# Two scan steps of a pair as one scan of 1024 columns, in the tiles in which a sequence begins

## The reference

```python
def _selective_scan(u, delta, A, Bm, Cm, D_param):
    def step(h, inp):
        delta_t, B_t, C_t, u_t = inp
        dA = jnp.exp(delta_t[:, :, None] * A[None])
        dBu = (delta_t * u_t)[:, :, None] * B_t[:, None, :]
        h = dA * h + dBu
        y_t = jnp.einsum('bdn,bn->bd', h, C_t)
        return (h, y_t)
    ...                       # h starts at zero in each sequence
    return y + u * D_param[None, None, :]

x = _layernorm(x + lightning_attention(x))   # layer 0, gated, 16 heads
x = _layernorm(x + ffn_0(x))                 # silu(x W1) * (x W3), Hadamard, W2
x = _layernorm(x + _selective_scan(...))     # layer 1, 32 states for each feature
x = _layernorm(x + ffn_1(x))                 # silu gate, 512 -> 2048 -> 512
```

## Time and profile before

| | us |
|---|---|
| median of 3 runs | 1828.31 (1827.86 to 1829.96) |
| profiled execution, its own time | 1820.48 |
| its span, first to last instruction | 1818.7 |
| scans of tile 0, first start to last start | 538.6 to 803.5 |
| first start of a scan in tile 1 | 808.1 |
| scans of tile 2, first start to last start | 1087.3 to 1363.8 |
| PE busy | 1736.3 (95%) |
| DVE busy | 1241.6 (68%) |
| mean granted clock of TensorE, share of full | 0.994 |

### The profile page before, as it was taken

How to read it: one execution, slowest core, us unless ns; L and a number is a source line. 1 busy time by engine, 2 the same in 40 slices (tenths; PEclk the granted TensorE clock), 3 DMA queues, 4 the chain that set the end, 5 groups by cost and what they waited for, 6 DMA issues and landing times. The chain is left out here.

```text
span 1818.7 us, 26882 instructions
## 1 busy us (share of the span) xinstructions
PE 1736.3 (95%) x9472; PEld 1134.8 (62%) x9472; DVE 1241.6 (68%) x1336; ACT 1120.5 (62%) x1721; POOL 1194.6 (66%) x932
## 2 busy tenths in 40 slices
PE   7999999799989999999999999998999999999998
PEld 5666666577756665565555665554656566667786
DVE  2524443323139999999899999987999999982212
ACT  5453443566577777867767777676776767653212
POOL 4634433355528877899887997788987988772111
PEclk9999999999999999999999999999999999999999
DMA  7443423487858987788776997777877787864652
GB/s 254 135 130 97 148 65 126 170 297 260 298 169 297 320 310 268 256 294 307 249 258 239 318 311 259 241 262 248 279 283 275 261 276 261 290 225 165 206 194 93
DMA packets 160023, 427.07 MB, mean 235 GB/s; under 512 B 31888, under 2 KB 54992, under 8 KB 159504
## 3 DMA queue, kind: packets, MB, share of 16 engines
q1 hardware_dynamic: 159888, 425.34, 68.6%
HBM read 356.07 MB, written 69.21 MB: 234 GB/s over the span
## 5 line engine op out<-in xcount | busy, mean ns | idle before, releaser
L1885 POOL TENSOR_TENSOR q_or_raw_or_h_times_c<-h_states,c_rep 128x512 f32<-128x512 f32 x293 | 375.5, 1296 | 50.0 <-DVE h_states L1775 45.2
L1650 ACT ACTIVATE decay<-delta_on_states,a_neg 128x512 f32<-128x512 f32 x512 | 350.2, 716 | 44.2 <-DMA delta_on_states<-delta 39.9
L1760 DVE TENSOR_TENSOR du_spread_in_d_b<-du_spread_in_d_b,b_rep 128x1024 f32<-128x1024 f32 x256 | 310.3, 1212 | 30.8 <-PE du_spread_in_d_b L1472 28.3
L1775 DVE TENSOR_TENSOR_SCAN h_states<-decay,h_last,du_spread_in_d_b 128x512 f32<-128x512 f32 x256 | 317.7, 1270 | 9.0 <-ACT h_last L1655 2.3
L1885 POOL TENSOR_TENSOR h_times_c_rest<-h_states,c_rep 128x512 f32<-128x512 f32 x219 | 282.2, 1300 | 55.7 <-DVE h_states L1775 47.6
L1775 DVE TENSOR_TENSOR_SCAN h_states<-decay,du_spread_in_d_b 128x512 f32<-128x512 f32 x256 | 302.2, 1209 | 18.4 <-ACT h_last L1655 12.3
L1837 POOL TENSOR_TENSOR h_lo<-v_or_silu_in_h_lo,h_hi 128x512 fp32r<-128x512 f32 x128 | 166.9, 1304 | 204.3 <-ACT h_hi L1552 203.3
L111 PE MATMUL y_or_aux<-h_hi,w 128*128 128x512 f32 x468 | 193.9, 414 | 10.9 <-POOL h_lo L1837 10.7
L1725 DVE TENSOR_TENSOR v_or_silu_in_h_lo<-v_or_silu_in_h_lo,up_or_scores 128x512 f32<-128x512 f32 x128 | 86.9, 679 | 146.0 <-PE up_or_scores L113 131.5
L113 PE MATMUL y_or_aux<-h_hi,w 128*128 128x512 f32 x468 | 183.4, 392 | 0.0
L112 PE MATMUL y_or_aux<-h_lo,w 128*128 128x512 f32 x468 | 182.8, 391 | 0.0
(11 more groups left out here) (240 smaller groups left out, 3840.0 us busy)
## 6 DMA issues: line engine op xcount, KB each, us to landing
delta_on_states<-delta SPq DMA_DIRECT2D x256, 512.0 KB, 5.8
w<-w_split SPq DMA_DIRECT2D x112, 512.0 KB, 5.6
attn_w_hi_or_x_hi_w<-w_split SPq DMA_DIRECT2D x112, 512.0 KB, 5.2
attn_w_lo_or_x_lo_w<-w_split SPq DMA_DIRECT2D x112, 512.0 KB, 5.4
w_split<-w_presplit_hi_lo SPq DMA_DIRECT2D x32, 512.0 KB, 4.0
w_presplit_hi_lo<-in_w13b SPq DMA_DIRECT2D x32, 256.0 KB, 3.5
w_split<-attn_w_hi_or_x_hi_w SPq DMA_DIRECT2D x8, 1024.0 KB, 6.6
w_split<-attn_w_lo_or_x_lo_w SPq DMA_DIRECT2D x8, 1024.0 KB, 6.6
```

Of the source, the lines that this page charges most:

```text
L1650: act.activation(da[:, s % ND], dring[:, s % NR], ACT.Exp, scale=a[:, column(s):column(s) + 1]).then_inc(s_da, 1)
L1760: dve.tensor_tensor(both, both, brep[:, tile_of(s // SPO) % 2].unsqueeze(1).to_broadcast([P, 2, TT]), ALU.mult).then_inc(s_db, 1)
L1775: dve.tensor_tensor_scan(hs[:, s % NH], da[:, s % ND], uu[:, s % NU], initial, ALU.mult, ALU.add).then_inc(s_hs, 1)
L1885: pool.tensor_tensor(hc[s % NC_], hs[:, s % NH], crep[:, tile_of(s // SPO) % 2], ALU.mult).then_inc(s_hc, 1)
```

## The change

In the tiles in which a sequence begins (0 and 2), one `tensor_tensor_scan` over 1024 columns, `scan_both`, takes the place of `scan(s)` and `scan(s+1)`. It stands where `scan(s)` stood, waits for both decays, for the `inject` of the pair, and for both slots of `hs`, and it raises the semaphore of the states by 2 when it ends. At the place of `scan(s+1)` only the `inject` is left. So that no state runs from the first half into the second, the decay of column 512, the first column of the odd step, has to be zero: ACT writes it for the three odd slots of `da` with a copy of one column (scaled by 0) at the first three odd steps of each of the two tiles, and the exp of an odd step then covers the other 511 columns. Tiles 1 and 3 keep `scan`. All 128 steps of tiles 0 and 2 become 64 instructions in each.

```diff
--- before.py
+++ after.py
@@ -1647,7 +1647,10 @@
                         act.wait_ge(s_dr[pair % (NR // 2)], 16 * (pair // (NR // 2) + 1))
                     if s >= ND:
                         act.wait_ge(s_hs, s - ND + 1)
-                    act.activation(da[:, s % ND], dring[:, s % NR], ACT.Exp,
+                    first = 0 if carried(s) else s % 2
+                    if first and s % (KD * SPO * TILES_PER_SEQ) < ND:
+                        act.activation(da[:, s % ND, 0:1], eps, ACT.Copy, scale=0.0)
+                    act.activation(da[:, s % ND, first:], dring[:, s % NR, first:], ACT.Exp,
                                    scale=a[:, column(s):column(s) + 1]).then_inc(s_da, 1)
 
                 def carry(s):
@@ -1775,9 +1778,22 @@
                     dve.tensor_tensor_scan(hs[:, s % NH], da[:, s % ND], uu[:, s % NU], initial,
                                            ALU.mult, ALU.add).then_inc(s_hs, 1)
 
+                def scan_both(s):
+                    dve.wait_ge(s_da, s + 2)
+                    dve.wait_ge(s_db, s // 2 + 1)
+                    if s >= NH:
+                        dve.wait_ge(s_hc, s - NH + 2)
+                        if keeps(s - NH):
+                            dve.wait_ge(s_ca, pairs_kept(s - NH))
+                    decays, inputs, states = (ring[:, s % n:s % n + 2].rearrange("p s t -> p (s t)")
+                                              for ring, n in ((da, ND), (uu, NU), (hs, NH)))
+                    dve.tensor_tensor_scan(states, decays, inputs, 0.0, ALU.mult, ALU.add).then_inc(s_hs, 2)
+
                 def step(s):
-                    if 0 <= s < STEPS:
+                    if 0 <= s < STEPS and carried(s):
                         scan(s)
+                    elif 0 <= s < STEPS and s % 2 == 0:
+                        scan_both(s)
                     if 0 <= s + 1 < STEPS and s % 2 == 1:
                         inject((s + 1) // 2)
                     if SPO <= s < STEPS and s % SPO == LAG + 1 or s == STEPS + LAG:
```

## The result

The changed kernel takes 1833.93 us (median of 10 runs, 1830.36 to 1837.04); the kernel before, timed beside it, 1828.0 us (10 runs, 1823.83 to 1833.74). The ratio is 1.0032 [1.0019, 1.0045], so 5.9 us or 0.3% more: slower, but little. A second comparison of the same two kernels gave 1.0044 [1.0027, 1.0061] (experiment 1). The square brackets hold the 95% interval. The forecast was 1828.9 us in a range of 1822.5 to 1834: the time lies in the range, 5 us above its likeliest value, and on the side that had a chance of 0.23. It lies outside the narrower range that the forecast mechanism had for itself (1826 to 1831.5).

What follows compares the result with a forecast made beforehand. PE was taken to set the pace, hiding DVE's saving. Terms 0.4 (late `hidden`), 0.3 (POOL), 0 (ACT's decays), 0 (zero column) and -0.1 (earlier DVE work) summed to +0.6 us, giving 1828.9 us, range 1822.5 to 1834.

Steps and rivals of the forecast that it cites:

- rival B: ACT's ten early decays wait for the joint scan and delay PE: slower, 7.5 us if PE stands for each; chance 0.20.
- Duration of the joint scan: On DVE, one scan of 1024 columns takes 2.28 us and lets its successor start after 2.19 us.
- DVE's saving: Joint scans save DVE 0.05 us a pair, 6.4 us over 128 pairs, hidden because PE is full.
- Later even states, later `hidden` and `add`: Even states, 18 `hidden` and 21 `add` come 1.07 us later; one up matmul waits, costing PE 0.4 us.
- POOL: POOL waits longer for even states; only the start of its tile 2 backlog moves, costing 0.3 us, between nothing and 1.07.
- ACT's decays: On ACT, ten early decays wait for the joint scan, 7.5 us together; taken as 0 since ACT has time to spare.
- Zero column: Six one-column copies on ACT in tiles 0 and 2, 1.1 us at most, beside idle time; taken as 0.
- What gets better: DVE reaches `inject` and the `add` that PE waited for 0.05 to 0.1 us sooner; taken as -0.1 us.
- A: DVE sets the pace and its saving shows: faster, 6.4 us off, 1822; chance 0.17.
- C: Later `hidden` and even states delay `h_low` and the products: slower, +5 us if a quarter show, 1833; chance 0.08.
- D, the forecast: PE sets the pace and little of the change shows; own range 1826 to 1831.5 us; chance 0.55.
- What the profile would show: Wrong if first scan of tile 0 to tile 1 changes over 2 us, or tile 2's stretch goes away or doubles.

Runs made afterwards that it cites:

- experiment 1: The changed kernel again, with no edit, against the kernel before: 1834.85 us, ratio 1.0044.
- Experiment 4: The changed kernel with two scans of 512 columns, each with its own increment, where the joint scan stands: 1831.58 us, ratio 1.0021 to the kernel before.
- experiment 10: The changed kernel with six tile 0 products (`step_size`, `step_input`, blocks 1 to 3) on POOL instead of DVE: 1828.58 us, ratio 1.0015 to the kernel before.
- experiments 8 and 9: First: kernel before, unaltered, one execution, 1830.05 us. Second: changed kernel, semaphore raised by 1, `hidden` and `add` ahead of the joint scan, 1832.58 us, ratio 1.0035.
- experiment 11: The kernel before with six tile 0 products (`step_size`, `step_input`, blocks 1 to 3) on POOL instead of DVE: 1827.19 us, ratio 1.0004 to the kernel before.
- experiment 12: The changed kernel with ACT issuing decays 2 steps ahead of the scan instead of 3: 1849.43 us, ratio 1.0125 to the kernel before.
- 5: The changed kernel with the joint scan raising its semaphore by 1 instead of 2: 1832.36 us, ratio 1.0025 to the kernel before.

## Why the prediction came out as it did

The sum, +0.6 us, was too small: the runs show +5.9, and +7.9 in the second comparison. The range held it because it reached for rival B's price, and no run shows that B's mechanism cost anything; that the time lay inside was luck as far as the mechanism goes.

- *Duration of the joint scan.* Right: 2.28 us forecast, 2283 ns measured; the next start 2.20 us later, 2.19 forecast.
- *DVE's saving.* What the joint scan itself takes was right, and what was missed stands ahead of it. The step looked at where the joint scan lets its successor start, not at how it starts itself. The raise by 2 puts a wait instruction in front of it, and a pair with `inject` right ahead that cycled in 3.55 us now needs 3.60. The busy time fell by 2.1 us, not 6.4, because the six products became longer as well (8.7 us in sum in this profile, 4.7 in the first of before). So the saving was not there to be hidden or shown.
- *Later even states, later `hidden` and `add`.* **This term was too small.** It asked, for each of the moved `hidden`, whether the up matmul would wait, and found one place with 0.4 us; experiment 1 shows 0.4 us there, the first profile after nothing. It didn't ask what else stands in DVE's order at the moved places. The `step_size` of blocks 1 to 3 stood between the two scans of a pair (steps 4, 12 and 20), so that 22 pairs of tile 0 and not 20 have something between them, and with `step_input` these products' length depends on what POOL does beside them. In the old order they took 0.67 to 0.95 us, once 1.89; in the changed kernel three of six took 1.3 to 4.0 in one profile and 1.3 to 1.5 in the other. Experiment 4 shows that the new order without the joint scan costs 0.0021 [0.0006, 0.0035], and experiment 10 that with these products off DVE tile 0 is as long as before. That it is their length beside POOL, and not their place in a full DVE, is not shown: by experiments 8 and 9 the stage doesn't follow their length. The prediction drew on what the Trainium skill says of DVE's fixed cost and not on what it says of the shared access to SBUF, which bears on these six.
- *POOL: 0.3 us.* Too small. Waits for states in tile 0 went from 12.5 to 28.4 us (25.9 in experiment 1), and behind them in POOL's program stood `h_low` (2.4 us of PE in one profile, 1.0 in the other). The claim that tight quads lie only in POOL's backlogs in tile 2 failed in tile 0, where PE now waits 0.6 us for a quad at 583; in tile 2 a second quad waits 0.6 at 1147. Tile 2's 1.4 to 1.6 us are close to the latter and the 0.9 for the second `add`; that these are its cause is read from lists of waits, and no experiment took them away. A tile 2 with the scans of before also took 280.3 us once (experiment 11), so that this difference is hardly clear of the scatter.
- *ACT's decays: 0, with 7.5 as the other end (rival B).* The waits came as foretold in place, 0.8 us in tile 0 and 4.2 in tile 2 instead of 7.5. There are five in tile 2, where nine were counted. What they cost is open: experiment 12 couldn't tell. The wait of the joint scan for the odd decay, put at nothing, stood 0.8 us in tile 0 and 0.6 in tile 2; no run prices it.
- *Zero column: 0.* Nothing in the trace stands for it.
- *What gets better: -0.1.* Not seen as such; the `add` behind line 1445 has two waits, 0.8 us together, in place of one of 1.0 in tile 0, and 1.9 in place of 1.0 in tile 2.
- *Rivals.* A is out: no version with the joint scan is faster than before, not even with DVE's cycle mended (5). C came nearest: later `hidden` and even states delay `h_low` and the products, at a price of 5 us. It had 0.08. Its mechanism was named without `step_size` and `step_input`. D, the forecast, had PE's pace right (busy 268 of 274 us in tile 0) and the size of what passes through to PE wrong.
- *What the profile would show.* The test "wrong if tile 0 changes by over 2 us" struck: 269.5 became 274.2 and 273.1. The stretch 1198 to 1258 stayed.

How much each part has of the 6 to 8 us is not settled. That tile 0's 3.0 to 4.7 us go away with the six products off DVE is shown by one profile (experiment 10), and the step in the median by intervals that touch or overlap; through which wait they act is argued. Tile 2's share has no experiment that takes it away. The two tiles alone give equal shares (0.0017, 0.0016), though the profiles of the changed kernel give tile 0 more. None of the versions with the joint scan beats the kernel before; the nearest, experiment 10, is 0.15% behind it.

## What to carry to other kernels

When an edit moves work in an engine's order, list everything in that order that shifts, and for each instruction whose length depends on a neighbour (here products of two SBUF operands on DVE beside POOL) look at what the neighbour does at the new time. A saving of 0.05 us for each instruction is easily used up at its own start: look in the trace whether the merged instruction still starts as soon after the one before it. And take a second profile before a stall is called the cause: the 3.98 us product was the largest item of the first one, and in the second it was 1.51 with the loss still there. Slack of an engine over a whole tile doesn't tell who stands behind a late item in its queue.

## What the hardware showed that wasn't expected

- A product of 128x512 with both inputs in SBUF lasted 0.67 us on DVE alone and up to 3.98 beside three POOL products in a row; it ended 0.55 us after the last of them. With nearly the same start beside POOL's `h_low` (0.34 us behind it, 0.35 in the other profile) one POOL product passed in experiment 1 and three in the first profile after. POOL's own product beside it lasted 1.75 instead of 1.29 when DVE had come first.
- A scan that raises its semaphore by 2 started 1.40 us after an `inject` began, one that raises it by 1 started 1.30 us after.
- Behind one scan of 1024 columns the next instruction started after 2.20 us, behind two of 512 after 2.24. The fixed part of an instruction, 0.135 us by the durations of products of 512 and 1024 columns, is worth some 0.05 us in start-to-start time, where each instruction starts before the one ahead has ended.
